# A fused transformer block on one core: tile 4 of the softmax weights transposed by VectorE and DRAM instead of TensorE, with reordered queues

## What is computed

```python
h = layernorm(x) * (1 + ca) + sa                       # x is 1024 x 512
q, k = rope(h @ wq), rope(h @ wk)                      # 32 query heads, 8 key and value heads, width 128
scores = q @ k.T / sqrt(128), causal mask, softmax     # 1024 x 1024 for each query head
x = x + ga * (softmax @ (h @ wv)) @ wo
h = layernorm(x) * (1 + cb) + sb
x = x + gb * (h @ W.T + b + low_rank_of_the_routed_rank(h))
```

## Time and profile before

| | |
|---|---|
| median of 3 runs | 1076.05 us (1075.98 to 1079.7) |
| the profiled execution | 1078.03 us, its span 1076.2 us |
| granted TensorE clock | 0.997 of full speed |
| TensorE busy, weight loads busy | 97%, 81% |
| VectorE busy | 73% |
| ScalarE busy | 59% |
| GpSimd busy | 49% |
| DMA | 26.7% of 16 engines, 86.92 MB |

### The profile page before, as it was taken

The page is one execution under the profiler, slowest core; times in us unless marked ns, Lnnn a source line. Parts: engine busy times, 40 slices in busy tenths (PEclk is TensorE's granted clock), DMA queues, the critical chain, the costliest instruction groups (busy, mean ns, idle before and its releaser), DMA issues.

```text
span 1076.2 us, 16548 instructions
## 1 busy us (share of the span) xinstructions
PE 1046.2 (97%) x5426; PEld 866.6 (81%) x5426; DVE 790.1 (73%) x1834; ACT 631.1 (59%) x1294; POOL 527.6 (49%) x510
## 2 busy tenths in 40 slices
PE   6999999999999999999999999999999999999997
PEld 3668888888888888888888888887888888887775
DVE  5678875787668875687758876688758876687566
ACT  5456763577347764477437664478437764476433
POOL 4536563456436563365435653365535653364234
PEclk9999999999999999999999999999999999999999
DMA  8362323122402323123302233123302233032001
GB/s 309 91 201 82 100 74 79 60 79 88 108 1 70 112 74 79 59 79 90 85 24 69 89 98 79 46 84 94 86 25 70 79 95 92 35 94 70 1 20 60
DMA packets 98285, 86.92 MB, mean 81 GB/s; under 512 B 39380, under 2 KB 84052, under 8 KB 98072
## 3 DMA queue, kind: packets, MB, share of 16 engines
q1 hardware_dynamic: 97384, 85.75, 26.7%
q10 hardware_dynamic: 816, 0.10, 0.1%
HBM read 59.23 MB, written 26.61 MB: 80 GB/s over the span
## 4 chain that ended last, share of the span: by engine, by line
PE 53%; DVE 15%; ACT 14%; POOL 9%; issue 6%; DMA 2%; SPq 1%; POOLq 0%; DVEq 0%; ACTq 0%
PE accumulators L709 16%; PE accumulators L694 14%; PE accumulators L675 7%; PE scores L625 6%; ACT p_large L934 6%; DVE p_large L1231 4%; PE transposed L638 4%; POOL p_small L1608 3%; DVE pb_lo L1243 3%; POOL qc L1621 2%; DVE p_small L1231 2%; POOL qr L1617 2%; PE scores L899 2%; DVE turned L1257 2%; ACT pa_hi L948 2%
## 5 line engine op out<-in xcount | busy, mean ns | idle before, releaser
L1608 POOL TENSOR_SCALAR p_large<-p_large,rowinv 128x640 f32<-128x640 f32 (+3 forms) x128 | 125.4, 980 | 225.9 <-DVE rowinv L1236 225.9
L942 ACT ACTIVATE pb_hi<-transposed 128x512 fp32r<-128x512 f32 (+3 forms) x256 | 118.8, 510 | 132.1 <-PE transposed L638 131.4
L1617 POOL TENSOR_TENSOR qr<-qr,trig 128x512 f32<-128x512 f32 x80 | 103.5, 1294 | 170.2 <-ACT qr L967 170.2
L934 ACT ACTIVATE p_large<-p_large,negmax 128x640 f32<-128x640 f32 (+3 forms) x128 | 126.4, 988 | 102.2 <-DVE negmax L1231 101.4
L1243 DVE TENSOR_TENSOR pb_lo<-transposed,pb_hi 128x512 fp32r<-128x512 f32 (+3 forms) x256 | 141.5, 584 | 28.1 <-ACT pb_hi L942 28.1
L1608 POOL TENSOR_SCALAR p_small<-p_small,rowinv 128x128 f32<-128x128 f32 (+3 forms) x128 | 96.8, 772 | 91.0 <-DVE rowinv L1236 91.0
L625 PE MATMUL scores<-k_hi,q_hi 128*128 128x512 f32 (+2 forms) x384 | 139.4, 363 | 0.0
L1231 DVE CUSTOM_DVE_ANT_0 p_large<-scores,mask 128x640 f32<-128x640 f32 (+3 forms) x128 | 130.0, 1015 | 9.9 <-PE scores L625 6.4
L625 PE MATMUL scores<-k_hi,q_lo 128*128 128x512 f32 (+2 forms) x384 | 131.4, 342 | 0.0
L625 PE MATMUL scores<-k_lo,q_hi 128*128 128x512 f32 (+2 forms) x384 | 131.1, 341 | 0.0
L1621 POOL TENSOR_TENSOR qc<-qc,qr 128x512 f32<-128x512 f32 x80 | 123.9, 1548 | 6.3
(11 more groups left out here) (181 smaller groups left out, 2281.0 us busy)
## 6 DMA issues: line engine op xcount, KB each, us to landing
p_rows<-turned SPq DMA_DIRECT2D x31, 640.0 KB, 2.9
pa_lo<-p_rows SPq DMA_DIRECT2D x124, 160.0 KB, 3.1
stage<-in_L_attn_wq_dram SPq DMA_DIRECT2D x32, 256.0 KB, 2.8
stage<-in_L_attn_wo_dram SPq DMA_DIRECT2D x32, 256.0 KB, 3.0
v_rows<-vt SPq DMA_DIRECT2D x32, 128.0 KB, 2.8
v_lo<-v_rows SPq DMA_DIRECT2D x32, 128.0 KB, 3.2
y<-in_L_wmod_dram SPq DMA_DIRECT2D x4, 512.0 KB, 6.7
stage<-in_L_attn_wk_dram SPq DMA_DIRECT2D x8, 256.0 KB, 2.7
```

The costliest lines, as they stand in the source:

```text
L934: nc.scalar.activation(row(i), row(i), ACT.Exp, bias=negmax[:, i:i + 1], scale=-1.0, accum_out=rowsum[:, i:i + 1]).then_inc(s_exp, 1)
L942: nc.scalar.activation(pt_of(i, part, True), src, ACT.Copy).then_inc(t_hi, 1)
L1608: nc.gpsimd.tensor_scalar(row(i), row(i), rowinv[:, i:i + 1], 1.0, ALU.mult, ALU.mult).then_inc(s_norm, 1)
L1617: nc.gpsimd.tensor_tensor(qr[:, s, :], qr[:, s, :], trig[:, 1, half * HALF:(half + 1) * HALF], ALU.mult).then_inc(r_sin, 1)
```

## The change

Tile 4 of each head but the last goes the way of tiles 0 to 3, in a roundtrip of its own: VectorE turns it in 32 x 32 blocks into the first 640 columns of `turned` (`turn_four`), once `p_rows` has left that buffer. SyncE sends it to `four_rows` in DRAM and back into `pb_lo`. ScalarE makes the hi part (`four_hi`) and VectorE the lo part (`four_lo`) in front of the next head. TensorE no longer transposes tile 4 (31 of 32 heads). `pb_hi` and `pb_lo` become `[128, 4, 29, 32]`, by query sub-block, so that all matmuls of `weighted(h, 1)` read their moving operand in runs of 32 elements, and the copies from PSUM write such runs. In the last head tile 4 is still transposed by TensorE.

Orders are changed too: VectorE makes the masks of tiles 4 and 5 in one go in places 1 to 3 and inverts row 4 before `output_lo`; `early_lo` and `early_hi` stand ahead of the rotated query in place 2; `transposed_hi` and `transposed_lo` of tile 6 stand ahead of the last filler in places 1 and 2; GpSimd normalises tile 6 between the two halves of the rotation in place 2. In the first group SyncE issues two modulation loads ahead of the roundtrips. The tail's order has small changes. The core of the diff:

```diff
 def turn_count(n, i):
-    return len(TURNS) * n + (1, 2, 4, 6)[i]
+    return (len(TURNS) + 1) * n + (1, 2, 4, 6, 7)[i]
...
-        pb_hi, pb_lo = sb("pb_hi", [P, 29, P], F32R), sb("pb_lo", [P, 29, P], F32R)
+        pb_hi, pb_lo = sb("pb_hi", [P, 4, 29, 32], F32R), sb("pb_lo", [P, 4, 29, 32], F32R)
...
+            def turn_four(n):
+
+                sp.wait_ge(p_turned, turn_count(n, 4))
+                if n:
+                    sp.wait_ge(four_in, 64 * n)
+                sp.dma_start(four_rows, turned[:, 0:5 * P]).then_inc(four_out, 16)
+                sp.wait_ge(four_out, 16 * (n + 1))
+                if n:
+                    sp.wait_ge(a_full, N.of[("a", ("pvb", (n - 1) % R), (n - 1) // R)])
+                src = four_rows.rearrange("(a c) (b m) -> b c a m", a=4, b=4)
+                for b in range(4):
+                    dst = f32(four_blocks(pb_lo)[32 * b:32 * b + 32]).rearrange("p a l r -> p a (l r)")
+                    sp.dma_start(dst, src[b]).then_inc(four_in, 16)
...
                 load(("q", 3), at)
                 turn_columns(R * g + 1)
+                turn_four(R * g + 1)
                 load(("wo", 1), at)
                 load(("wo", 2), at)
                 turn_columns(R * g + 2)
+                turn_four(R * g + 2)
...
+                    n = head_number(h, at, ahead) + 1
+                    if n <= LAST:
+                        pe.wait_ge(four_hi_done, n)
                 for done, count, products, keys in steps:
                     pe.wait_ge(done, count)
+                    if half and done is t_lo and count == first and n <= LAST:
+                        pe.wait_ge(four_lo_done, n)
...
                 fill(h, 4, at)
-                transposes(h, 4, at)
                 scores(h, 6, at)
...
+            def four_hi(h, at, ahead):
+
+                n = head_number(h, at, ahead)
+                act.wait_ge(four_in, 64 * (n + 1))
+                nc.scalar.activation(four_blocks(pb_hi), f32(four_blocks(pb_lo)), ACT.Copy).then_inc(four_hi_done, 1)
...
                     output_hi(hb, 0, at, ahead)
+                    four_hi(hb, at, ahead)
                 fill(h, 1, at)
...
+                elif i == 6 and head_number(h, at) < LAST:
+                    row_free = (p_turned, turn_count(head_number(h, at), 4))
...
+            def turn_four(h, at):
+
+                n = head_number(h, at)
+                need(dve, s_norm, N.value("s", (h, 4), at))
+                dve.wait_ge(rows_out, 16 * (n + 1))
+                nc.vector.transpose(four_turned.rearrange("p b l r -> p l b r"),
+                                    row(4).rearrange("p (j b c) -> p j b c", b=4, c=32)).then_inc(p_turned, 1)
+
+            def four_lo(h, at, ahead):
+                dve.wait_ge(four_hi_done, head_number(h, at, ahead) + 1)
+                nc.vector.tensor_tensor(four_blocks(pb_lo), f32(four_blocks(pb_lo)), f32(four_blocks(pb_hi)),
+                                        ALU.subtract).then_inc(four_lo_done, 1)
...
-                transposed_lo(h, 4, at)
+                if at.first and not h:
+                    fill(h, 4, at, slice(-1, None))
+                turn_four(h, at)
                 masked(h, 6, at)
```

More of the change, by code:

```diff
@@ L839, in _ @@
             scores(3, 6, G7)
+            transposes(3, 4, G7)
             weighted(3, 0, G7)
[L841 removed]
             weight_transposes(2)
@@ L1373, in front @@
                 if h or not at.first:
+                    four_lo(hb, at, ahead)
                     transposed_lo(hb, 7, at, ahead)
```

99 lines of the change are left out of this document (58 added, 41 removed).

## The result

| | before | after |
|---|---|---|
| median of 8 runs | 1076.9 us (1075.72 to 1079.7) | 1071.9 us (1067.52 to 1074.12) |
| ratio, 95% interval | | 0.9948 (0.993 to 0.9966) |
| profiled execution, its span | 1078.03, 1076.2 us | 1074.12, 1072.3 us |
| bytes moved by DMA | 86.92 MB | 107.22 MB |

The change gains 5 us where 26 were forecast; 1071.9 lies above the range of 1039 to 1064. The sign was right, the size was not.

What follows compares the result with a forecast made beforehand. TensorE was taken as full in places 0 and 3, a chain through TensorE, VectorE, ScalarE and GpSimd as the bound in place 2. 17.0 + 14 - 5 = 26 us off 1076.05 gave 1050 us, range 1039 to 1064.

Steps and rivals of the forecast that it cites:

- 17.0 us off TensorE: Tile 4's transposes leaving TensorE: 0.55 us a head in 31 heads, taken in full as 17.0 us gained.
- The lower end of the term: Transposes' gain in places 0 and 3 only, where TensorE is full: 8.3 us, all on the path.
- 14 us for the order of waits: Earlier masks and splits on VectorE shorten TensorE's waits: 60% of 23.4 us, mostly in places 1 and 2.
- The layout at nothing: Late-half matmuls and PSUM copies using runs of 32: 2 us at most, taken as nothing.
- VectorE's load at nothing: VectorE gains net 0.6 to 0.8 us a head, covered by idle time in place 2; no cost taken.
- `four_lo` at 5 us for its collisions: `four_lo` overlapping GpSimd's rotations in places 0 and 2: 0.3 us in 16 heads, 5 us back.
- A full lock in every such head: Upper bound for `four_lo` and GpSimd locking each other out: 1.1 us in 15 or 16 heads, 17 us.
- The DMAs covered: Tile 4's roundtrip of 7.8 us lands before `four_hi` needs it, covered by about 0.9 us; no cost.
- The first group, plus or minus 2: Two modulation loads ahead of the first roundtrip may make VectorE wait once: nothing, plus or minus 2 us.
- the signs that the prediction named: Profile after: place 0 head 0.3 to 0.6 us shorter, place 2 at 22.0 to 22.5, division waits about 10 us.
- B: Rival: VectorE becomes the bound in places 1 and 2, lengthening those heads: 1070 to 1079 us, chance 0.09.
- rival A: Only the transposes are gained, as new late links replace old ones: 1059 to 1064 us, chance 0.22.

Runs made afterwards that it cites:

- e5: Changed kernel, new orders and layout kept, with nothing done for tile 4 in 31 heads (no turn, DMAs or splits; zeros in the product): 1044.94 us.
- f1: Changed kernel with `four_lo` moved ahead of the front's filler and the mask of tile 2 in places 0 and 1: 1067.41 us.
- e6: Kernel before with the new orders alone, tile 4 still on TensorE in the old layout: 1070.21 us.
- e1: Kernel before, old orders, with tile 4's transposes and both splits left out in 31 heads: 1069.07 us.
- e2: Changed kernel with `four_lo` left out, an empty instruction raising its semaphore: 1053.58 us.
- f2: f1 plus `four_lo` behind tile 3's mask and three inverses in places 2 and 3, and TensorE's late-half hi products before the lo ones: 1060.06 us.
- e3: Changed kernel with tile 4's five DMAs issued in the first head only: 1070.49 us.
- e4: Changed kernel with the old orders on VectorE, ScalarE and GpSimd, layout by sub-block kept: 1083.43 us.
- g2: f2 with `four_hi` of place 2 moved ahead of the query's swap: 1065.48 us.
- g3: f2 with, in place 3, exp 5 ahead of the key weights' split, and query filler and row 5's inverse ahead of their lo split: 1065.1 us.
- h2: Changed kernel with the first group's two modulation loads issued behind the roundtrip of tiles 0 to 3, as before: 1072.58 us.

## Why the prediction was wrong

**17.0 us off TensorE: right as work, wrong as a gain of this kernel.** Place 0 shows it cleanly: 43.37 before, 42.81 in e5 and f1, 0.56 where 0.55 was worked out. With the new orders in place it is so everywhere: from e6 to e5 the four places lose 0.54, 0.62, 0.54 and 0.63. The lower end of the term, 8.3 us in places 0 and 3 where TensorE is full and "it is all on the path", was no lower end: in the changed kernel place 0 is at 43.43 and place 3 at 31.47. A full TensorE had not meant that VectorE's results came with time to spare, and `four_lo` made them late.

**14 us for the order of waits: not a size that any run shows.** e6 gives 7 us, with tile 4 on TensorE; e5 is 24 faster than e1, with tile 4 gone from both. By their traces 18.5 of these 24 lie between the starts of the second and the last head, 2.0 ahead of them and 3.4 behind, where e5 also has the change's order of loads and its tail. So the term has no value of its own, and that the sum of 31 met the 32 of e5 is in part luck. What the runs do show is that neither part gives its gain without the other, 8 + 7 against 32: while one strand of the chain is late, shortening the other gives little.

**The layout at nothing: right.** The late and early matmuls of 512 columns against v_lo take 394 and 398 ns, 393 and 397 before. And place 0 without tile 4 is as long with the new layout as with the old (42.81 in e5, 42.78 in e1).

```profile
L699 PE MATMUL accumulators<-pb_hi,v_lo 128*128 128x512 f32 x160 | 47.4, 394 | 0.0
L699 PE MATMUL accumulators<-pa_hi,v_lo 128*128 128x512 f32 x32 | 12.7, 398 | 0.0
```

**VectorE's load at nothing, and `four_lo` at 5 us for its collisions: this is the step that failed.** The durations were right (0.84 for the turn of 640 columns, 0.82 for `four_lo`, 1.14 beside a rotation), and so was the collisions' share, about 6 us; the price was not. The sum had no term for the instruction itself. The prediction added up the load of a head and found 3 us of slack in place 2. But the slack lies at the end of the chain of masks and in front of `qc`; `four_lo` was put where there is none, ahead of the mask of tile 3 on which five further steps hang. I noted that it "stands ahead of the splits of tile 7" and covered it by TensorE's 8 hi products, that is by the wait of its own consumer, and not by what was queued behind it. Even the consumer waits: the product needs tile 7's splits too, and they come behind `four_lo`. e2 puts the price at 18.3 us in place of 5. f1 wins back 4.5 of them by its place alone, and f2 11.8 in all. In f2 part of this is the end of the collisions, which the new place brings too, and TensorE's new order of products may have a share; these were not taken apart.

The load itself rose by less than the 0.6 to 0.8 us a head that were worked out: 14.6 us in 31 heads are 0.47. Other splits met GpSimd less often; `pa_lo` fell from 1.73 us in the mean to 1.56 and `wo_lo` from 0.85 to 0.67.

Of the lock between VectorE and GpSimd ("SBUF — State Buffer", "Who interferes with whom", in the Trainium skill) the trace again agrees in kind, 1.14 against 0.81 us; f2 moved the instruction out of the rotation's way and the excess is gone. A full lock in every such head, the 17 us that the rule was carried to, did not come: the excess here was 0.33 us, and the sum of the rotation beside it lasted 1.28.

**The DMAs covered: right for tile 4.** ScalarE never waits at `four_hi`, and by the medians e3 gains 1.4 us. Two waits did appear that I had not named. They are DMA waits of the changed kernel (us in total, times, longest):

```profile
ACT pa_hi L971 <- DMA pa_lo<-p_rows: 8.6, 8, 2.0
DVE turned L1299 <- DMA p_rows<-turned: 8.0, 15, 1.9
```

The first is tiles 0 to 3's own roundtrip in place 2, whose `early_hi` was moved forward; the second is the turn of tile 4, which needs `turned` to be empty. e3 has both as well (5.1 and 10.2 us), so the added traffic is not what brings them, though the first is 3.5 us less there; e6, with the same orders and tile 4 on TensorE, has neither, e5 the first (4.0 us), in heads that are shorter, and e4, with the old orders, not the first. That the shorter head is what brings the first is my reading and wasn't tested.

**The first group, plus or minus 2: at its edge, and it hides a price.** Against the kernel before, the second head begins 2.1 us later and the fifth 1.8 (153.0 instead of 151.2). Against e5, which has nothing for tile 4, the second head begins 5.3 later, 4.8 in e2. In the changed kernel TensorE waits there behind the gate products, for a result that VectorE reaches late, since it works from the turn (at 61.17, behind the write) to that result almost without a pause:

```profile
70.29 1.99 PE L718 MATMUL accumulators<-h_hi,wq_hi 128*128 128x512 f32 x4 [3.10 <-DVE ga_b L1391]
```

Of the 27 us that the new way costs over e5, 18.3 are `four_lo`. Of the other 8.7, by the two traces, roughly half fall in this first head and most of the rest in places 2 and 3 (0.16 and 0.25 us a head, some 3 us). The turn and the DMAs were not taken away one by one behind e2, so how this rest divides between them stays open.

**The rivals.** Of the signs that the prediction named, place 2 came (22.27 us) and place 0 did not (43.43, none of the 0.3 to 0.6 off). B's interval, 1070 to 1079, holds the result, but not by B's mechanism: place 2 was to become longer and became 0.6 us shorter, with VectorE idle for 3.5 us. What happened is rival A's, "a new late link at each place where an old one goes, say GpSimd's division or `four_lo` ahead of tile 7", with its sign: the waits of the transposes' weight loads for GpSimd stayed at 21.1 us, 23.4 before. A kept the 17 us of the transposes and took at most 5 off, which is the same failed step; so its range, 1059 to 1064, missed too.

```profile
L657 PEld LDWEIGHTS transposed<-ident,p_large 128*128 128x128 f32 x677 | 76.7, 140 | 27.1 <-POOL p_large L1663 21.1
```

The rule to keep such transposes on TensorE (the Trainium skill, "VectorE: DVE Perf Modes", "Rules for kernel authors") came out better than I gave it credit for: with the new orders, tile 4 on TensorE (e6) takes 1070.2 and on VectorE 1071.9, which can't be told apart. Only with `four_lo` at another place and TensorE's new order of products (f2) does the move pay, by 10 us.

## What to carry to other kernels

The added instruction cost what waited behind it in its engine's list, not its share of that engine's idle time (18.3 us, where 5 were taken). Before adding one, name the next instruction behind it that another engine waits for, and look for the hole (here 2.76 us in front of `qc`) where it delays nobody.

Where several strands have nearly one length, two shortenings can each show little and together much (8 and 7, but 32), and a repair of the wait that the profile names can lengthen the kernel (g2, g3). A wait that a profile names also says only where the chain is late: e5, the fastest kernel of all, still has 1.05 us from the last score to tile 5's transposes in place 3, about as much as the changed kernel's 1.17. So test a removal together with the reordering, and take the kernel with neither part nor price (e5) as the mark of what is to be had.

A stretch in which TensorE is 100% busy is not one in which it alone decides.

## What was not expected of the hardware

The write of 640 KB from `turned` took 3.6 us in h2, with no modulation load ahead of it, and 8.6 us in the changed kernel, behind two loads of modulation weights. So a roundtrip's price in one head says little of another's. The executions of the changed kernel also spread more, 6.6 us in 8 runs against 4.0 before. The first head alone differed by 3.7 us between four traces with the same lists up to its end (74.7 to 78.4), so part of the spread may lie there; its cause stays open.
